# Moving the third set of table rows, one query load and the running maxima inside the prologue of a relative-position attention kernel

## The chip, the cores and the metric

One core of a Trainium2 chip runs the whole program. The metric is the device time of the program in microseconds, the median over runs. The engines are PE (TensorE), DVE (VectorE), ACT (ScalarE), POOL (GpSimd) and SP (SyncE, which here does nothing but issue DMAs). Each runs its own list of instructions in order; semaphores order them against each other and against the 16 DMA engines.

## The reference, cut to what matters

A decoder layer on x (4 x 1024 x 256): self-attention with 16 heads of 16 and clipped relative positions, cross-attention to a context of 154 rows, and a gated feed-forward part with quantised weights; each is added to its input and normalised. The change touches only the self-attention:

```python
q, k, v = proj(Wq, bq), proj(Wk, bk), proj(Wv, bv)
attn = einsum('bhld,bhrd->bhlr', q, k) * scale
dist = clip(arange(L)[None, :] - arange(L)[:, None], -64, 8) + 64
rel = einsum('bhld,lrd->bhlr', q, dist_emb[dist]) * scale
out = einsum('bhlr,bhrd->bhld', softmax(attn + rel), v)
```

## The kernel before, in words

The self-attention has 16 groups of four heads (`NIT`, index i, four for each batch entry) and each is done in two half groups T = 2i and 2i + 1 of 512 queries, so there are 32 half groups. All work before the half groups is the prologue, and the change lies in it.

The prologue goes over 8 blocks k of 512 rows of x (`BLKS`), and in each over six products n: two for q (n = 0, 1), two for k (2, 3), two for v (4, 5). A product (k, n) is written (4, 2) and so on below. `project` is PE's part. For n < 4, ACT makes the high bf16 part (`high`), DVE the remainder (`remainder`), ACT the middle part, POOL the low part (`low`), and SP stores the three parts to DRAM with two DMAs of 192 KB (`store_part`; L268, and L270 for small wrapped pieces of 3 KB in even blocks). For v, ACT copies, POOL adds the bias and SP stores 544 KB (`store_values`). PE has two PSUM banks for this, so a product waits for DVE (`a_rem`) or ACT (`a_vc`) to have read the one two before it. The SBUF buffers of parts and values are double: `high(k, n)` waits until the stores of block k - 2 have landed.

Between the products stands the early work of the first half groups:

- `load_q(i)`, four DMAs of 768 KB together, brings the stacked parts of q of group i; `load_k`, `load_v` and `load_max_operands` bring the other operands.
- Rows (T, j), j = 0 to 3: PE multiplies q by the position embedding (`make_row`, L810; it waits for `load_q` of group T // 2), ACT copies, POOL pads, SP stores 400 KB to a table in DRAM (`store_row`, L326). When all four have landed, `load_windows(T)` reads them back skewed, in four DMAs of 400 KB (L318).
- Chunks (T, c), c = 0 to 15: PE multiplies q and k roughly (`max_chunk`, L836 and L837, into one of two banks) and DVE takes maxima with the window added (`chunk`, L710 to L715; the first of a half group waits for its window). 24 chunks are done in the prologue, 16 for T = 0 and 8 for T = 1.
- `shift_of(T)` on POOL, `turn_shift(T)` on PE and `place_shift(T)` on SP (L331) turn the maxima of a half group into three extra rows of q. Half group 0 can't begin without them.

The tables `rows_after` and `chunk_after` say behind which product a row or a chunk stands, on every engine alike. SP's list is written out by hand. In before it goes through blocks 3 and 4 with `load_windows(0)`, `load_q(1)`, the rows of T = 1, `load_windows(1)` and the rows of T = 2 in between, then stores blocks 5 and 6, and then issues `place_shift(0)`, `load_windows(2)`, `load_max_operands(1)`, `load_v(0)` and the stores of block 7, in this order. Behind that begins the loop over half groups. In its first half group PE needs `place_shift(0)` for the first score (`scores`, L866), and `load_v(0)` for the first product with v (`weigh`, L884), which stands behind the scores of two key tiles.

Of the kernel before, what the change touches and what calls it, by code (L numbers as in the profile page):

```python
# [45 lines left out]
def self_attention(nc, sem, ad, xT, wqT, wkT, wvT, bq, bk, bv, emb, part_of_row, e_lo, e_hi, ident,  # L46
# [17 lines left out]
    BLKS = 2 * B  # L64
# [5 lines left out]
    with ctx:  # L70
# [149 lines left out]
        steps = [(k, n) for k in range(BLKS) for n in range(6)]  # L220
        rows_after = {s_: (0, j) for j, s_ in enumerate(((2, 4), (2, 5), (3, 0), (3, 1)))}
        rows_after.update({(3, 2 + j): (1, j) for j in range(4)})
        rows_after.update({(4, 2 + j): (2, j) for j in range(4)})
        first_chunks = [(0, c) for c in range(CH)] + [(1, c) for c in range(LEAD)]
        chunk_after = dict(zip(steps[steps.index((4, 0)):], first_chunks))
        SHIFT_STEP = (7, 0)

        def chunks_of(T, kt):

# [7 lines left out]
        def q_slot(i):  # L237
            return i % QS
# [5 lines left out]
        def _(sp):  # L244
# [16 lines left out]
            def store_part(k, n):  # L261
                b, hf = k // 2, k % 2
                cols = slice(hf * HALF, (hf + 1) * HALF)
                sp.wait_ge(a_low, 4 * k + n + 1)
                for gg in range(2):
                    dst = (qd, kd)[n // 2][4 * b + 2 * (n % 2) + gg].rearrange("t r h n -> (r h) t n")
                    src = part[gg * G * HD:(gg + 1) * G * HD, hf, n]
                    sp.dma_start(dst[:, :, cols], src).then_inc(st_part[hf][n], 16)  # L268
                    if n >= 2 and hf == 0:
                        sp.dma_start(dst[:, :, L:L + WRAP], src[:, :, 0:WRAP]).then_inc(st_part[hf][n], 16)  # L270

            def store_values(k):
                b, hf = k // 2, k % 2
                cols = slice(hf * HALF, (hf + 1) * HALF)
                sp.wait_ge(a_v, 2 * k + 2)
                sp.dma_start(vd[b, cols].rearrange("(t p) c -> p t c", p=P), vs[:, hf].rearrange("p t h r -> p t (h r)")).then_inc(st_val[hf], 16)
                if hf == 0:
                    sp.dma_start(vd[b, L:L + WRAP], vs[0:WRAP, hf, 0].rearrange("p h r -> p (h r)")).then_inc(st_val[hf], 16)

            def three(t, i, p0, p1, lo, hi):  # L280

                return t[i, p0:p1].rearrange("t r h n -> (t r) h n")[:, :, lo:hi]

            def load_q(i):
                q, s = qT[:, q_slot(i)], ld_q[q_slot(i)]
                sp.dma_start(q[0:16], three(qd, i, 0, 1, 0, L)).then_inc(s, 16)
                sp.dma_start(q[16:48], three(qd, i, 0, 2, 0, L)).then_inc(s, 16)
                sp.dma_start(q[48:80], three(qd, i, 1, 3, 0, L)).then_inc(s, 16)
                sp.dma_start(q[80:96], three(qd, i, 0, 1, 0, L)).then_inc(s, 16)
# [62 lines left out]
            def store_parts(k, *projections):  # L352
                for n in projections:
                    store_part(k, n)

            def store_rows(T, *tiles):
                for j in tiles:
                    store_row(T, j)
# [17 lines left out]
            store_parts(3, 1)  # L376
            sp.wait_ge(s_pads, 16 * 2 * ENDS)
            load_windows(0)
            load_q(1)
            store_rows(1, 0)  # L380
            store_parts(3, 2)
            store_rows(1, 1)
# [2 lines left out]
            store_values(3)  # L385
            store_parts(4, 0, 1)
            load_windows(1)
            store_rows(2, 0)
            store_parts(4, 2)
            store_rows(2, 1)  # L390
            store_parts(4, 3)
            store_rows(2, 2, 3)
            store_values(4)
            load_k(0)
            sp.wait_ge(s_bufs, 1 + 2 * G)
            for par in range(2):
                sp.dma_start(kT[99:102, par, :, (TL - 1) * P:L - WRAP], none[0:3, :, 0:P - WRAP]).then_inc(s_wrap, 16)
            for k in range(5, BLKS - 1):
                store_parts(k, 0, 1, 2, 3)
                store_values(k)  # L400
            place_shift(0)
            load_windows(2)
            load_max_operands(1)
# [53 lines left out]
        def _(pool):  # L457
# [12 lines left out]
            def low(k, n):  # L470

                hf = k % 2
                pool.wait_ge(a_mid, 4 * k + 1 + n)
                nc.gpsimd.tensor_tensor(part[:, hf, n, 2, :], rem[:, hf, n, :], part[:, hf, n, 1, :], ALU.subtract).then_inc(a_low, 1)  # L474
# [48 lines left out]
            for k, n in steps:  # L523
                if (k, n) == (0, 4):
                    pool.wait_ge(s_const, 16 * NCONST)
                    pool.wait_ge(s_ones, 1)
                if n < 4:
                    low(k, n)
                else:
                    add_value_bias(k, n - 4)  # L530
                if (k, n) in rows_after:
                    pad_row(*rows_after[k, n])
                if (k, n) == (6, 4):
                    shift_of(0)
                    fill_ends(0)
                    cut_window(0)
# [20 lines left out]
        def _(act):  # L557
# [66 lines left out]
            for k, n in steps:  # L624
# [8 lines left out]
                if (k, n) in rows_after:  # L633
                    copy_row(*rows_after[k, n])
                if (k, n) == SHIFT_STEP:
                    copy_shift(0)
# [18 lines left out]
        def _(dve):  # L655
# [40 lines left out]
            def chunk(T, c):  # L696

                q4, h, n = c // G, c % G, CH * T + c
                qt = 4 * (T % 2) + q4
                a, z = max(0, qt * P - LEFT), min(L, qt * P + P + RIGHT)  # L700
                u = a - (qt * P + RIGHT - P)
                bank = psX[:, n % 2, :]
                if c == 0:
                    dve.wait_ge(ld_w[T % NW], 16 * G * (T // NW + 1))
                    if T >= 2:
                        dve.wait_ge(m_top, T - 1)
                if n >= 2:
                    dve.wait_ge(x_read, n - 1)
                dve.wait_ge(x_full, n + 1)
                last = nc.vector.tensor_tensor_reduce(junk[:, n % 2, 0:z - a], bank[:, a:z], win[:, T % NW, q4, h, u:u + z - a],  # L710
                                                      1.0, NEG, ALU.add, ALU.max, mx[:, T % 2, q4, h, 1:2])
                if a > 0:
                    last = nc.vector.tensor_reduce(mx[:, T % 2, q4, h, 0:1], bank[:, 0:a], AX.X, ALU.max)  # L713
                if z < L:
                    last = nc.vector.tensor_reduce(mx[:, T % 2, q4, h, 2:3], bank[:, z:L], AX.X, ALU.max)  # L715
                last.then_inc(x_read, 1)
                if c == CH - 1:
                    dve.wait_ge(x_read, n + 1)
                    nc.vector.tensor_tensor(mx[:, T % 2, :, :, 3], mx[:, T % 2, :, :, 0], win[:, T % NW, :, :, FLAT], ALU.add).then_inc(m_left, 1)
                    if T:  # L720
                        dve.wait_ge(m_ready, T)
                    dve.wait_ge(m_left, T + 1)
                    nc.vector.tensor_reduce(shift[:, 0], mx[:, T % 2].rearrange("p q h s -> p (q h) s")[:, :, 1:4], AX.X, ALU.max).then_inc(m_top, 1)
# [19 lines left out]
            for k, n in steps:  # L743
                if n < 4:
                    remainder(k, n)
                if (k, n) == (0, 5):
                    dve.wait_ge(s_const, 16 * NCONST)
                    prepare_embedding()
                    nc.vector.memset(none[:], 0.0).then_inc(s_bufs, 1)
                if k in (2, 3) and n < 4:  # L750
                    ones_row(k - 2, n)
                if (k, n) in chunk_after:
                    chunk(*chunk_after[k, n])
            dve.wait_ge(a_vc, 2 * BLKS)
            nc.vector.memset(psO[:], 0.0).then_inc(s_bufs, 1)
            for T in range(NT):
# [13 lines left out]
        def _(pe):  # L770
# [57 lines left out]
            def max_chunk(T, c):  # L828
                i, q4, h, n = T // 2, c // G, c % G, CH * T + c
                if c == 0:  # L830
                    pe.wait_ge(ld_q[q_slot(i)], q_loads(i))
                    pe.wait_ge(ld_x[i % 2], 16 * 7 * (i // 2 + 1))
                if n >= 2:
                    pe.wait_ge(x_read, n - 1)
                lo = T % 2 * HALF + q4 * P
                mm(psX[:, n % 2, 0:HALF], qT[0:64, q_slot(i), h, lo:lo + P], kX[0:64, i % 2, h, :], start=True, stop=True)  # L836
                mm(psX[:, n % 2, HALF:L], qX[64:128, i % 2, h, lo:lo + P], kX[64:128, i % 2, h, :], start=True,  # L837
                   stop=True).then_inc(x_full, 1)
# [49 lines left out]
            for k, n in steps:  # L888
                project(k, n)
                if (k, n) == (2, 4):  # L890
                    pe.wait_ge(s_prep, 3)
                if (k, n) in rows_after:
                    make_row(*rows_after[k, n])
                if (k, n) in chunk_after:
                    max_chunk(*chunk_after[k, n])
                if (k, n) == SHIFT_STEP:
                    turn_shift(0)
            pe.wait_ge(a_rem, 4 * BLKS)
# [1179 lines left out]
```

## Time and profile before

| what | value |
|---|---|
| median of 3 runs | 1418.46 us (1417.92 to 1419.0) |
| the profiled execution, own time | 1418.14 us |
| its span, first to last instruction | 1416.4 us |
| PE busy | 89% of the span |
| DVE, ACT, POOL busy | 75%, 69%, 25% |
| prologue, up to the first score | 129.1 us |
| half groups 0 to 31 | from there to about 960 us |

In the page's picture of the span in 40 slices of 35.4 us, PE shows 9 or more tenths from slice 5 on to slice 27, and 7 to 8 in the first four. The DMA engines show 7 to 9 tenths in the first five slices, more than in any later slice. A DMA share near 1.1 in the views below is a full queue, since packets of one DMA engine overlap.

### The profile page before, as it was taken

To read this page: it belongs to the slowest core of one execution; us is meant where nothing else is said; L and a number is where in the kernel's file an instruction comes from. 1 tells how busy PE (TensorE), PEld (TensorE's weight loads), DVE (VectorE), ACT (ScalarE), POOL (GpSimd) and SP (SyncE) were. 2 spreads that over 40 slices of the span, in tenths; PEclk is the share of its full clock that TensorE was granted. 3 is DMA by queue.
4 is the path that set the end of the run, shared out by engine and by line. 5 is a ranking of instruction groups with operands and counts; after the bars stand their busy time and mean duration, and the time that the engine had idled before them with its cause. 6 is when DMAs were issued, how large, how long until landed. Compare 5 with 4: busy or idle time off the path is not lost. (4 is left out here: it accounts for less than half of the span.)

```text
span 1416.4 us, 25656 instructions
## 1 busy us (share of the span) xinstructions
PE 1257.9 (89%) x8540; PEld 672.4 (47%) x8540; DVE 1057.2 (75%) x2561; ACT 974.5 (69%) x1690; POOL 352.5 (25%) x587
## 2 busy tenths in 40 slices
PE   7788999999999999999999999999997699930397
PEld 4344344334334334334434434436886588720397
DVE  3366788888887888888888888872564466999687
ACT  4434777777777777777777777772676458969672
POOL 4544121211211211212112112014463002410033
PEclk9989999999999999999999999999998899975699
DMA  8999877777777687587686685625320322837023
GB/s 221 287 305 265 204 178 202 187 183 199 185 198 188 176 216 184 158 229 182 169 219 177 186 199 156 186 79 174 103 77 34 116 89 79 276 121 267 0 90 119
DMA packets 263761, 243.02 MB, mean 172 GB/s; under 512 B 69294, under 2 KB 246990, under 8 KB 259534
## 3 DMA queue, kind: packets, MB, share of 16 engines
q1 hardware_dynamic: 261998, 238.24, 61.7%
q10 hardware_dynamic: 1632, 3.15, 0.7%
q8 instruction: 68, 1.11, 0.3%
q14 instruction: 63, 0.52, 0.1%
HBM read 139.01 MB, written 101.53 MB: 170 GB/s over the span
## 5 line engine op out<-in xcount | busy, mean ns | idle before, releaser
L618 ACT ACTIVATE pr<-scoresT 128x512 f32<-128x512 f32 x1024 | 548.4, 600 | 205.7 <-PE scoresT L871 148.9
L866 PE MATMUL scoresT<-qT,kT 99*128 99x512 bf16 (+9 forms) x1536 | 357.4, 313 | 4.8 <-issue 2.3
L715 DVE TENSOR_REDUCE mx<-scores_for_max 128x1 f32<-128x888 f32 (+6 forms) x448 | 301.6, 673 | 0.0
L710 DVE CUSTOM_DVE_ANT_0 junk<-scores_for_max,win 128x200 f32<-128x200 f32 (+2 forms) x512 | 179.9, 351 | 152.9 <-PE scores_for_max L837 144.2
L713 DVE TENSOR_REDUCE mx<-scores_for_max 128x1 f32<-128x64 f32 (+6 forms) x448 | 277.4, 619 | 0.0
L884 PE MATMUL attn_out<-pr,vS 128*17 128x512 f32 x2048 | 270.3, 600 | 2.5 <-DMA vS<-v_all 2.3
L866 PEld LDWEIGHTS scoresT<-qT,kT 99*128 99x128 bf16 (+1 forms) x1536 | 113.2, 98 | 334.0 <-ACT rows L595 97.0
L871 PE MATMUL scoresT<-idf,win 128*128 128x128 f32 (+1 forms) x1024 | 199.6, 256 | 0.0
L836 PE MATMUL scores_for_max<-kX,qT 64*128 64x512 bf16 x512 | 167.8, 386 | 3.9 <-DVE mx L715 3.0
L484 POOL COPY rows<-rows 128x512 f32<-128x512 f32 x128 | 78.6, 614 | 361.3 <-ACT rows L595 361.3
L837 PE MATMUL scores_for_max<-kX,qX 64*128 64x512 bf16 x512 | 167.8, 386 | 0.0
L871 PEld LDWEIGHTS scoresT<-idf,win 128*128 128x128 f32 (+1 forms) x1024 | 128.1, 143 | 19.2 <-issue 0.5
L2003 PE MATMUL banks<-w_gate_high,x_high 128*128 128x256 f32 x128 | 36.8, 288 | 82.5 <-DVE x_low L1925 82.4
L1869 DVE TENSOR_REDUCE amax<-raw 128x1 f32<-128x3072 f32 (+2 forms) x26 | 80.6, 3100 | 5.9 <-ACT raw L1772 5.6
L836 PEld LDWEIGHTS scores_for_max<-kX,qT 64*128 64x128 bf16 x512 | 35.9, 94 | 100.7 <-issue 47.2
L2003 PEld LDWEIGHTS banks<-w_gate_high,x_high 128*128 128x128 f32 x128 | 25.2, 197 | 83.1 <-issue 82.8
L595 ACT ACTIVATE rows<-scoresT 128x288 f32<-128x288 f32 x128 | 54.2, 424 | 10.8 <-DMA rel_table<-rows 10.2
L1772 ACT ACTIVATE raw<-banks,step 128x512 f32<-128x512 f32 x48 | 33.1, 689 | 29.2 <-PE banks L1978 29.2
L810 PE MATMUL scoresT<-embS,qT 96*128 96x72 bf16 x512 | 37.9, 196 | 16.8 <-DMA qT<-q_parts 10.4
L474 POOL TENSOR_TENSOR shared<-rem,shared 128x512 bf16<-128x512 f32 x32 | 36.8, 1157 | 59.0 <-ACT shared L571 58.9
L884 PEld LDWEIGHTS attn_out<-pr,vS 128*17 128x17 f32 x2048 | 34.0, 95 | 34.4 <-ACT pr L618 10.5
L519 POOL TENSOR_TENSOR shared<-ov,orec 128x256 f32<-128x256 f32 x16 | 10.0, 623 | 148.1 <-PE scoresT L866 106.8
(219 smaller groups left out, 2005.5 us busy)
## 6 DMA issues: line engine op xcount, KB each, us to landing
rel_table<-rows SPq DMA_DIRECT2D x128, 400.0 KB, 4.1
win<-rel_table SPq DMA_DIRECT2D x128, 400.0 KB, 5.0
up_raw<-xT_normed SPq DMA_DIRECT2D x6, 1536.0 KB, 10.3
xT_normed<-up_raw SPq DMA_DIRECT2D x6, 1536.0 KB, 6.4
qT<-q_parts SPq DMA_DIRECT2D x32, 256.0 KB, 7.1
kX<-k_parts SPq DMA_DIRECT2D x64, 128.0 KB, 4.1
kT<-k_parts SPq DMA_DIRECT2D x32, 256.0 KB, 4.8
q_parts<-shared SPq DMA_DIRECT2D x32, 192.0 KB, 4.5
```

Source lines behind the costliest of these rows:

```text
L484: nc.gpsimd.tensor_copy(rows[:, j, :, 0:LP], rows[:, j, :, LP:LP + 1].to_broadcast([P, G, LP])).then_inc(r_padded, 1)
L618: nc.scalar.activation(pr[:, n % NPR, h, :], bank, ACT.Exp).then_inc(t_read, 1)
L710: last = nc.vector.tensor_tensor_reduce(junk[:, n % 2, 0:z - a], bank[:, a:z], win[:, T % NW, q4, h, u:u + z - a], 1.0, NEG, ALU.add, ALU. ...
L713: last = nc.vector.tensor_reduce(mx[:, T % 2, q4, h, 0:1], bank[:, 0:a], AX.X, ALU.max)
L715: last = nc.vector.tensor_reduce(mx[:, T % 2, q4, h, 2:3], bank[:, z:L], AX.X, ALU.max)
L836: mm(psX[:, n % 2, 0:HALF], qT[0:64, q_slot(i), h, lo:lo + P], kX[0:64, i % 2, h, :], start=True, stop=True)
L837: mm(psX[:, n % 2, HALF:L], qX[64:128, i % 2, h, lo:lo + P], kX[64:128, i % 2, h, :], start=True, stop=True).then_inc(x_full, 1)
L866: last = mm(bank[:, a:e], k[0:r], q[0:r, a:e], start=(n == 0), stop=not near and n == len(pieces) - 1, skip_group_check=True)
L871: last = mm(bank[:, a:e], rel, idf[0:e - a, 0:e - a], is_transpose=True, start=False, stop=n == len(near) - 1, skip_group_check=True)
L884: last = mm(psO[32 * h:32 * h + VW, :], vS[:, i % 2, kt, VW * h:VW * (h + 1)], pr[:, n % NPR, h, :], start=(kt == 0), stop=(kt == TL - 1))
L1869: nc.vector.tensor_reduce(amax[:, k, n:n + 1], src, AX.X, ALU.max, apply_absolute_value=True).then_inc(done, 1)
L2003: mm(to(n, q), oh[m // 2][:, c], wdh[:, d], start=(m == 0 and q % 2 == 0), stop=False, skip_group_check=True)
```

## The change

It moves work between places of the prologue and leaves every instruction as it is.

- `rows_after`: the four rows of T = 2 stand behind the products (6, 2) to (6, 5) in place of (4, 2) to (4, 5).
- Chunks: they begin behind (4, 4) in place of (4, 0). At (5, 4), (5, 5), (6, 4) and (6, 5) two are done in place of one, so that all 24 are still done by (7, 5).
- `SHIFT_STEP` and POOL's `shift_of(0)` come one product later, (7, 1) and (6, 5).
- SP: `load_q(1)` stands behind `load_k(0)`, in front of the stores of block 5, in place of behind `load_windows(0)`. The four `store_row(2, j)` stand among the stores of the second half of block 6, the last of them right in front of `place_shift(0)` and `load_windows(2)`.

```diff
-        rows_after.update({(4, 2 + j): (2, j) for j in range(4)})
+        rows_after.update({(6, 2 + j): (2, j) for j in range(4)})
-        chunk_after = dict(zip(steps[steps.index((4, 0)):], first_chunks))
-        SHIFT_STEP = (7, 0)
+        TWICE = [(k, n) for k in (5, 6) for n in (4, 5)]
+        chunk_steps = sorted(steps[steps.index((4, 4)):] + TWICE)
+        chunks_after = {s_: [c for at, c in zip(chunk_steps, first_chunks) if at == s_] for s_ in chunk_steps}
+        SHIFT_STEP = (7, 1)
...
             load_windows(0)
-            load_q(1)
             store_rows(1, 0)
...
             load_windows(1)
-            store_rows(2, 0)
-            store_parts(4, 2)
-            store_rows(2, 1)
-            store_parts(4, 3)
-            store_rows(2, 2, 3)
+            store_parts(4, 2, 3)
             store_values(4)
             load_k(0)
...
-            for k in range(5, BLKS - 1):
-                store_parts(k, 0, 1, 2, 3)
-                store_values(k)
+            load_q(1)
+            store_parts(5, 0, 1, 2, 3)
+            store_values(5)
+            store_parts(6, 0, 1, 2)
+            store_rows(2, 0)
+            store_parts(6, 3)
+            store_rows(2, 1, 2)
+            store_values(6)
+            store_rows(2, 3)
             place_shift(0)
             load_windows(2)
...
-                if (k, n) == (6, 4):
+                if (k, n) == (6, 5):
                     shift_of(0)
```

PE in block 4, before: behind the first product of k, (4, 2), stands the first row of T = 2 (`embS,qT`), which waits for `load_q(1)` (`ld_q1`), and a chunk (`scores_for_max`).

```order
L788 MATMUL scoresT<-xs,wk 128x512 [waits a_rem]
L788 MATMUL scoresT<-xs,wk 128x512
L810 MATMUL scoresT<-embS,qT 128x72 [waits t_read,ld_q1]
L810 MATMUL scoresT<-embS,qT 128x72 x3
L836 MATMUL scores_for_max<-kX,qT 128x512 [waits x_read]
L837 MATMUL scores_for_max<-kX,qX 128x512
L788 MATMUL attn_out<-xs,wk 128x512 [waits a_rem]
```

PE at the same place, after: the products of q and k in block 4 follow each other, and the first chunk stands behind (4, 4).

```order
L791 MATMUL scoresT<-xs,wk 128x512 [waits a_rem]
L791 MATMUL scoresT<-xs,wk 128x512
L791 MATMUL attn_out<-xs,wk 128x512 [waits a_rem]
L791 MATMUL attn_out<-xs,wk 128x512
L796 MATMUL scoresT<-wv,xs 128x256 [waits a_rem]
L796 MATMUL scoresT<-wv,xs 128x256 x3
L839 MATMUL scores_for_max<-kX,qT 128x512 [waits ld_x0,ld_q0]
```

Nothing that waits for `ld_q1` is left in block 4.

SP behind the stores of block 6, before: the last store of k's parts, the values, then the shift and the third window.

```order
L268 DMA k_parts<-shared 64x3x512
L270 DMA k_parts<-shared 64x3x8
L276 DMA v_all<-vs 128x4x272 [waits a_v]
L278 DMA v_all<-vs 8x272
L331 DMA qT<-sh 6x512 [waits t_read]
L331 DMA qT<-sh 6x512 x3
L318 DMA win<-rel_table 128x4x200 [waits st_row2,st_row3,st_row1,st_row0]
```

SP at the same place, after:

```order
L328 DMA rel_table<-rows 128x4x200 [waits ld_w0,r_padded] x2
L278 DMA v_all<-vs 128x4x272 [waits a_v]
L280 DMA v_all<-vs 8x272
L328 DMA rel_table<-rows 128x4x200 [waits ld_w0,r_padded]
L333 DMA qT<-sh 6x512 [waits t_read]
L333 DMA qT<-sh 6x512 x3
L320 DMA win<-rel_table 128x4x200 [waits st_row2,st_row3,st_row1,st_row0]
```

The rows of T = 2 now stand here, and the third window waits for the landing of a store that is issued just ahead of it.

## Rows read from the trace of the kernel before

**Rows 1.** The page, its first line and the busy times.

```profile
span 1416.4 us, 25656 instructions
PE 1257.9 (89%) x8540; PEld 672.4 (47%) x8540; DVE 1057.2 (75%) x2561; ACT 974.5 (69%) x1690; POOL 352.5 (25%) x587
```

**Rows 2.** Waits, 60 to 240 us: us in total, times, longest.

```profile
DVE junk L710 <- DMA win<-rel_table: 7.7, 1, 7.7
...
PE scoresT L810 <- DMA qT<-q_parts: 9.2, 1, 9.2
...
PE scoresT L866 <- issue: 2.3, 1, 2.3
PE attn_out L884 <- DMA vS<-v_all: 2.3, 1, 2.3
```

**Rows 3.** Timeline of block 4: start, us, engine, line; idle before and releaser.

```profile
64.64 1.98 PE L788 MATMUL scoresT<-xs,wk 128*128 128x512 f32 x4
...
72.12 0.30 DVE L710 CUSTOM_DVE_ANT_0 junk<-scores_for_max,win 128x136 f32<-128x136 f32 x1 [7.72 <-DMA win<-rel_table]
...
75.81 0.42 PE L810 MATMUL scoresT<-embS,qT 96*128 96x72 bf16 x4 [9.18 <-DMA qT<-q_parts]
```

**Rows 4.** Timeline, products on PE: two of block 1, two of block 6.

```profile
18.57 1.88 PE L788 MATMUL scoresT<-xs,wq 128*128 128x512 f32 x4
...
20.29 1.88 PE L788 MATMUL attn_out<-xs,wq 128*128 128x512 f32 x4
...
101.87 1.98 PE L788 MATMUL attn_out<-xs,wq 128*128 128x512 f32 x4
...
104.11 1.98 PE L788 MATMUL scoresT<-xs,wk 128*128 128x512 f32 x4
```

**Rows 5.** Timeline, two chunks in a row on DVE, their first instructions.

```profile
112.21 0.37 DVE L710 CUSTOM_DVE_ANT_0 junk<-scores_for_max,win 128x200 f32<-128x200 f32 x1
...
113.49 0.35 DVE L710 CUSTOM_DVE_ANT_0 junk<-scores_for_max,win 128x200 f32<-128x200 f32 x1
```

**Rows 6.** Stretches: us, PE, PEld, DVE, ACT, POOL busy, clock, DMA share, GB/s.

```profile
66.00:114.00 48.00, 38.82 (x136) 18.66 (x135) 31.34 (x80) 17.91 (x31) 22.11 (x24) 0.89 1.09 317
114.00:122.00 8.00, 8.00 (x27) 2.79 (x25) 6.29 (x16) 3.59 (x6) 5.33 (x8) 1.00 0.80 213
122.00:124.00 2.00, 2.00 (x10) 1.44 (x8) 1.79 (x6) 1.58 (x3) 0.92 (x2) 1.00 0.06 13
```

**Rows 7.** Stretches with TensorE's granted clock (last but two), same columns.

```profile
72.00:76.00 4.00, 0.20 (x4) 0.20 (x4) 3.83 (x8) 0.63 (x1) 1.15 (x1) 0.50 0.99 249
76.00:82.00 6.00, 6.00 (x19) 2.57 (x17) 1.94 (x4) 1.84 (x4) 0.14 (x1) 0.52 1.11 324
...
140.00:150.00 10.00, 10.00 (x55) 3.51 (x53) 5.13 (x13) 5.44 (x11) 0.85 (x2) 0.67 0.86 200
```

**Rows 8.** Timeline of SP: start, us spent on issuing.

```profile
62.55 2.55 SPq L318 DMA_DIRECT2D win<-rel_table  x4
...
83.17 2.40 SPq L318 DMA_DIRECT2D win<-rel_table  x4
...
109.55 3.64 SPq L268 DMA_DIRECT2D q_parts<-shared  x4
113.24 0.66 SPq L268 DMA_DIRECT2D k_parts<-shared  x1
...
119.73 2.99 SPq L331 DMA_DIRECT2D qT<-sh  x4
122.90 2.02 SPq L318 DMA_DIRECT2D win<-rel_table  x4
...
129.50 0.38 SPq L310 DMA_DIRECT2D vS<-v_all  x1
```

**Rows 9.** Timeline, PE's first score and first product with v.

```profile
129.09 0.38 PE L866 MATMUL scoresT<-qT,kT 99*128 99x200 bf16 x2 [2.31 <-issue]
...
138.16 1.05 PE L884 MATMUL attn_out<-pr,vS 128*17 128x512 f32 x8 [2.31 <-DMA vS<-v_all]
```

**Rows 10.** The row stores, 40 to 145 us: issue to landing.

```profile
DMA to landing us min/median/max: 4.6/6.3/10.4
```

More of the change, by code:

```diff
@@ L751, in _ @@
                     ones_row(k - 2, n)
-                if (k, n) in chunk_after:
-                    chunk(*chunk_after[k, n])
+                for c in chunks_after.get((k, n), ()):
+                    chunk(*c)
             dve.wait_ge(a_vc, 2 * BLKS)
@@ L893, in _ @@
                     make_row(*rows_after[k, n])
-                if (k, n) in chunk_after:
-                    max_chunk(*chunk_after[k, n])
+                for c in chunks_after.get((k, n), ()):
+                    max_chunk(*c)
                 if (k, n) == SHIFT_STEP:
```

## The prediction

> **What bounds the kernel now.** I read the page first, then the waits, then the stretches and the timeline of the prologue, SP's row of the timeline last. The page [rows 1] says that PE is busy 89% of the span; in the slices of the page between the prologue and the end of the half groups it is 9 tenths or more. The change leaves all that work alone, so it can win only what PE loses before the half groups run, and the question is by how much the point moves from which PE runs without a stop.
>
> The waits of this part [rows 2] name three losses of PE: 9.2 us for `load_q(1)`, 2.3 us at the first score, 2.3 us for `load_v(0)`. The first is what the change goes at. In the timeline [rows 3] PE makes the product (4, 2) at 64.64, then sits until 75.81 before the first row of T = 2. DVE sits 7.7 us too, until the first window lands at 72.12, and the maxima of the first chunk and the remainder of (4, 1) are queued behind it. After the stop the clock is at half (granted 0.50 and 0.52, the 1.2 GHz level) up to 82 us [rows 7].
>
> PE isn't the only thing that is full here. From 66 to 114 us the DMA engines have a share of 1.09 and move 317 GB/s; from 114 to 122 the share is 0.80 and the rate 213; from 122 to 124 nearly nothing moves [rows 6]. SP shows why: it issues without a pause from 109.55 to 122.9 [rows 8], about 0.65 us for each DMA, and eight of the last ones before 119.7 are the small wrapped pieces of k and the values, four more are the shift. So up to 114 the queue is bound by what it moves, and then for 9 us by SP.
>
> The last wait sets the end. The first score comes at 129.09, and the first product with v at 138.16, released by the DMA of vS [rows 9]. That load is issued at 129.50, behind `load_windows(2)` at 122.90 and `load_max_operands(1)` [rows 8]. From the issue of window 2 to PE's release are 138.16 - 122.90 = 15.3 us. Whatever PE gains earlier, it waits there.
>
> **Removed: the wait for `load_q(1)`, and with it what PE did late.** From the product (4, 2) at 64.64 there are 22 products to the end of the prologue. One alone takes 20.29 - 18.57 = 1.72 us, one with a chunk 104.11 - 101.87 = 2.24 us, so a chunk adds 0.52 [rows 4]. With four rows at 0.15 (an estimate from their four short products) PE needs 22 x 1.72 + 24 x 0.52 + 0.6 = 50.9 us and ends at about 115.5. In before it ends at 126.8 (129.09 less 2.31 idle). That is 11.3 us for PE alone: 9.2 of wait, the rest from the slow clock.
>
> The part buffers could hold this back, since `high(k, n)` waits for the stores of two blocks earlier. Without the 768 KB of `load_q(1)`, which took the queue from 72.12 to 75.81, 3.7 us [rows 3], and without the four rows of T = 2 (1.6 MB, 5 us at 317 GB/s), the stores of block 4 come some 4 us earlier by the queue and k's 5 to 8; those of block 5 are again behind `load_q(1)`. By the queue's rate I put the first store of block 5 at about 103.5 landed, where ACT wants it at 103.3, and the later ones ahead of their use. I take a stall of 0 to 2 us, hidden by what follows.
>
> **Chunks doubled.** DVE takes 113.49 - 112.21 = 1.28 us for a chunk [rows 5]. In a block with two doubled steps it has 8 x 1.28 + 4 x 0.75 = 13.2 us of work, and PE 6 x 1.72 + 8 x 0.52 = 14.5. DVE lags by half a microsecond behind a doubled step and makes it up in the next. Cost 0 to 1 us in all, hidden as well. `turn_shift` and `shift_of` one product later cost nothing: SP gets to the shift at 113 or later, its data are ready by about 106.
>
> **The DMA queue, which is the sum.** All that the queue has to move before `load_windows(2)` is the same set of transfers in both kernels, since `load_q(1)` and the rows of T = 2 were moved ahead of that point within it, not past it. The queue is full from 66 us on. So it ends earlier only by the time in which it was not full. Between 114 and 122 it moved 8 x 213 = 1.70 MB, which at 317 GB/s is 5.4 us: 2.6 us idle in effect; by the share, 8 x (1.09 - 0.80) / 1.09 = 2.1 us. From about 122.0 to 122.9 it was empty, another 0.9 us [rows 6, 8]. In the changed kernel the rows of T = 2, 400 KB each, stand between the small pieces, so that the queue stays full while SP issues them. All data for them are there: the last row's product comes at about 101.5. SP's own time isn't in the way either: from the second window on (in after at about 79.6: 83.17 less 3.7) it has to issue some 35 us of DMAs and would end at 115. The queue then runs empty at 122.0 - 2.6 = 119.4.
>
> **The added wait.** `load_windows(2)` now waits for the row (2, 3), which is stored just ahead of the shift. Behind that wait on SP stand `load_max_operands(1)`, `load_v(0)` and all stores of block 7; PE's first product with v waits for them. With a full queue a row lands when the queue has got to it, so I count only its tail, 0 to 1.5 us, and take 0.5, as the median row lands 6.3 us after issue and SP is about that far ahead of the queue [rows 10]. Window 2 is then issued at 119.4 + 0.5 = 119.9, 3.0 us earlier than before. Ends: 2.1 - 0.6 = 1.5 us on the low side, 2.6 + 0.9 = 3.5 on the high one.
>
> Nothing behind window 2 changes, so vS lands at about 135.2. The shift lands at about 120, since its DMAs stand in the full queue; PE, ready at 115.5, starts the half group then, is at the first product with v at about 127 and waits 8 us there, in place of 2.3. Of the 11.3 us that PE gains 3.0 are left.
>
> **The clock behind that wait.** In before the clock falls after the 2.3 us of idle time: granted 0.67 from 140 to 150 [rows 7]. After the 9.2 us stop it was at half for 5.9 us of work, 75.8 to about 81.7. A wait of 8 us should be like the second, so I book the same loss for both kernels, and half a microsecond either way.
>
> **Sum.** 1418.14 of the profiled execution less 3.0 is 1415.1; it lies 0.3 under the median of the runs, so the forecast is **1415.4 us**. 0.2% of the time is 2.8 us, about what a measurement can tell from no change, so the forecast lies just outside of it.
>
> **Rivals.**
>
> A, *SP sets the end and not the queue*. If the queue catches up before block 6 ends, window 2 is issued when SP gets there, at 115 to 117, and the gain is 6 to 8 us: 1411. For it speaks that SP was what held the queue from 114 on [rows 6, 8]. Against it speaks the share of 1.09 over 48 us, and that the changed kernel has 1.6 MB more to move in just that stretch of SP's list. Chance 0.13. The Trainium skill, "Perfetto Trace Analysis", section "What 'DMA-bound' means", keeps two bounds apart: the DMA engines themselves, or the sequencer of the issuing engine, which then shows a solid track of DMA slices. SP's track is solid from 109.55 on, so by that rule this rival would be the forecast; the share of 1.09 up to 114 goes against it.
>
> B, *the queue loses as much as it gains*. The 8 KB packets of `load_q(1)`, moved next to `load_k(0)`, or a starved moment at the second window, which waits for the rows of T = 1, cost 1 to 2 us of rate; or the last row's tail is 1.5 us and more. Then 0 to 1.4 us are left: 1417 to 1418.5. Chance 0.17.
>
> C, *the wait for the last row takes the place of the removed one*: slower. The row (2, 3) is issued directly ahead of the shift. If SP gets there no earlier than it got to the shift in before (119.73 [rows 8]), the row is issued at 119.7, lands 6.3 us later [rows 10] at 126.0 to 126.6 with nothing else in the queue, window 2 is issued 3 to 4 us later than at 122.90, and the time is 1422. It decides if block 6 comes 6 us or more later than I have it, say by stalls on part buffers. Chance 0.08.
>
> D, *PE's whole gain stays*, 1407: only if vS landed by 127, for which its place in SP's list leaves no room. Below 0.01, and not counted.
>
> **Chances and range.** The forecast's own case, a gain of 2 to 5 us, has 0.62: 0.40 of it is beyond 0.2%, 0.22 within. With A, faster is 0.53; with B, same is 0.39; slower is 0.08. The own range is 1413.4 to 1416.5. The range to 1411.5 takes in half of A, and up to 1418.9 all of B; left out are C and the rest of A, about 0.15.
>
> **What would show it.** Right: no wait for `qT<-q_parts` in block 4, products at 1.7 to 2.0 us up to (4, 3), PE through with the prologue at 114 to 118, window 2 issued at 119 to 121, DMA share above 1 from 66 to 119, a wait of 6 to 9 us on vS before the first product with v, which comes at 134.5 to 136.5. Wrong: window 2 issued before 118 (A) or after 122 (B, C), PE stopped in blocks 5 to 7 by `st_part`, or a stop in half group 1 or 2 that before doesn't have.

## The result and the profile after

The changed kernel takes 1422.42 us (median of 19 runs, 1420.44 to 1425.17), the kernel before 1419.36 (median of 19, 1417.43 to 1422.66). The ratio is 1.0019, with a 95% interval of 1.0013 to 1.0026: slower by 0.19%, or 2.7 us (1.8 to 3.7). The forecast was 1415.4, and the range ended at 1418.9; both lie on the wrong side. The profiled execution took 1420.71 us with a span of 1418.9, against 1418.14 and 1416.4 before. The ratios below use fast executions alone; one of e1's twelve took 2400.79 us and is left out.

The page of the changed kernel, its first line and the busy times, answers [rows 1]. The number of instructions and the work are the same:

```profile
span 1418.9 us, 25656 instructions
PE 1255.3 (88%) x8540; PEld 672.2 (47%) x8540; DVE 1057.1 (75%) x2561; ACT 973.7 (69%) x1690; POOL 354.4 (25%) x587
```

PE's waits from 60 to 240 us (total, times, longest) answer [rows 2]:

```profile
PE scoresT L813 <- DMA qT<-q_parts: 9.8, 1, 9.8
PE attn_out L887 <- DMA vS<-v_all: 5.3, 1, 5.3
PE scoresT L869 <- issue: 2.3, 1, 2.3
PE scoresT L869 <- DMA qT<-sh: 1.0, 1, 1.0
```

The wait for the second stacked q is still there, and longer than the 9.2 us of before. It stands at another place, as PE's timeline shows (start, us; idle before it and releaser in brackets), which answers [rows 3]:

```profile
64.42 1.98 PE L791 MATMUL scoresT<-xs,wk 128*128 128x512 f32 x4 [0.22 <-DVE rem L696]
66.24 1.88 PE L791 MATMUL attn_out<-xs,wk 128*128 128x512 f32 x4
68.10 1.99 PE L796 MATMUL scoresT<-wv,xs 128*128 128x256 f32 x8
...
91.59 1.98 PE L791 MATMUL scoresT<-xs,wk 128*128 128x512 f32 x4
103.37 0.42 PE L813 MATMUL scoresT<-embS,qT 96*128 96x72 bf16 x4 [9.79 <-DMA qT<-q_parts]
103.72 0.60 PE L839 MATMUL scores_for_max<-kX,qT 64*128 64x512 bf16 x1
104.26 3.78 PE L791 MATMUL attn_out<-xs,wk 128*128 128x512 f32 x4
```

In block 4 the products now follow each other as forecast. PE is through with (6, 2) at 93.57, and the row behind it, the first one of T = 2, stands until 103.37. SP's timeline says why, and answers [rows 8]:

```profile
62.53 2.28 SPq L320 DMA_DIRECT2D win<-rel_table  x4
...
80.77 2.60 SPq L320 DMA_DIRECT2D win<-rel_table  x4
...
94.22 1.67 SPq L394 DMA_DIRECT2D kT<-no_shift  x2
95.94 0.42 SPq L288 DMA_DIRECT2D qT<-q_parts  x1
...
97.36 0.42 SPq L291 DMA_DIRECT2D qT<-q_parts  x1
97.83 2.63 SPq L270 DMA_DIRECT2D q_parts<-shared  x4
...
103.83 3.56 SPq L270 DMA_DIRECT2D q_parts<-shared  x4
110.60 0.57 SPq L270 DMA_DIRECT2D k_parts<-shared  x1
...
119.87 0.92 SPq L328 DMA_DIRECT2D rel_table<-rows  x1
120.83 3.33 SPq L333 DMA_DIRECT2D qT<-sh  x4
125.63 2.02 SPq L320 DMA_DIRECT2D win<-rel_table  x4
...
132.14 0.38 SPq L312 DMA_DIRECT2D vS<-v_all  x1
```

`load_q(1)` is issued from 95.94 on, 2.4 us after PE began to want it, and lands at 103.3. The same stop then reaches SP. It has issued the q parts of block 6 at 107.39 and stands until 110.60 for the k parts of (6, 2), although PE had made that product at 93.57. ACT and POOL tell where it lay:

```profile
93.67 0.69 ACT L569 ACTIVATE shared<-scoresT,colc 128x512 bf16<-128x512 f32 x1 [1.03 <-PE scoresT L791]
94.26 0.62 ACT L574 ACTIVATE shared<-rem 128x512 bf16<-128x512 f32 x1
103.82 0.41 ACT L598 ACTIVATE rows<-scoresT 128x288 f32<-128x288 f32 x1 [8.95 <-PE scoresT L813]
108.14 0.69 ACT L569 ACTIVATE shared<-attn_out,colc 128x512 bf16<-128x512 f32 x1 [3.90 <-PE attn_out L791]
108.72 0.62 ACT L574 ACTIVATE shared<-rem 128x512 bf16<-128x512 f32 x1
...
109.42 1.16 POOL L477 TENSOR_TENSOR shared<-rem,shared 128x512 bf16<-128x512 f32 x1 [13.31 <-ACT shared L574]
```

ACT makes the middle part of a product one product later, behind the copy of the row (L598) and the next high part. So the finished product (6, 2) waits for the row that waits for `load_q(1)`, and its store is issued 17 us after PE was done with it.

Four stretches answer [rows 6, 7] (PE, PEld, DVE, ACT and POOL busy, granted clock, DMA share, GB/s):

```profile
96.00:106.00 10.00, 2.63 (x8) 1.19 (x9) 1.37 (x4) 0.41 (x1) 0.10 (x1) 0.61 1.06 267
106.00:114.00 8.00, 7.86 (x41) 4.64 (x39) 4.77 (x14) 3.67 (x8) 4.58 (x6) 0.85 0.76 222
114.00:122.00 8.00, 8.00 (x26) 3.01 (x27) 7.49 (x21) 3.64 (x7) 6.09 (x11) 1.00 0.95 278
124.00:126.00 2.00, 2.00 (x11) 1.31 (x10) 1.99 (x6) 1.59 (x3) 1.50 (x2) 1.00 0.06 16
```

From 106 to 114 the queue has a share of 0.76: it ran dry while SP stood from 107.39 to 110.60 (0.12 from 110 to 112). After PE's stop the clock is at its lower level (1.2 GHz, granted 0.50 from 104.26 to 108.04), and the product (6, 3) takes 3.78 us in place of 1.98.

The end of the prologue answers [rows 9]:

```profile
130.25 0.38 PE L869 MATMUL scoresT<-qT,kT 99*128 99x200 bf16 x2 [2.32 <-issue]
141.13 1.91 PE L887 MATMUL attn_out<-pr,vS 128*17 128x512 f32 x8 [5.32 <-DMA vS<-v_all]
```

Window 2 is issued at 125.63 in place of 122.90, 2.7 us later, v's load with it, and the first product with v comes 3.0 us later. The first half group ends 2.6 us later than before, the last one 2.8. That is the result.

### The profile page after: what moved, and what is told of

The parts are those of the page before. It is cut to its first block and busy times, and to the rows that moved or that the text cites. A ratio compares the mean times of both kernels' runs of the same rounds, so it can differ in the third digit from the quotient of the medians.

```text
span 1418.9 us, 25656 instructions
## 1 busy us (share of the span) xinstructions
PE 1255.3 (88%) x8540; PEld 672.2 (47%) x8540; DVE 1057.1 (75%) x2561; ACT 973.7 (69%) x1690; POOL 354.4 (25%) x587
## 5 line engine op out<-in xcount | busy, mean ns | idle before, releaser
L598 ACT ACTIVATE rows<-scoresT 128x288 f32<-128x288 f32 x128 | 54.4, 425 | 17.8 <-PE scoresT L813 10.0
L813 PE MATMUL scoresT<-embS,qT 96*128 96x72 bf16 x512 | 37.9, 196 | 18.1 <-DMA qT<-q_parts 11.5
L477 POOL TENSOR_TENSOR shared<-rem,shared 128x512 bf16<-128x512 f32 x32 | 36.8, 1155 | 58.8 <-ACT shared L574 58.6
```

## The experiments

Two executions don't reach the prologue's middle at the same time, so places are compared as distances from the issue of the first window, in us. All are differences of starts in the timelines. "Half group 0 ends" is ACT's first copy of a half group's output. Ratios are to the kernel before in runs beside it, with 95% intervals. Each row of places is one profiled execution; e4 and e7 have the same SP list up to window 2 and differ there by 0.8 us (61.5 and 60.7), so a difference under 1 us is read as nothing unless a wait in the profile accounts for it.

| kernel | PE ends prologue | window 2 issued | first score | first product with v | half group 0 ends | ratio |
|---|---|---|---|---|---|---|
| before | 64.2 | 60.3 | 66.5 | 75.6 | 102.4 | |
| the change | 65.4 | 63.1 | 67.7 | 78.6 | 104.9 | 1.0019 [1.0013, 1.0026] |
| e1, q back | 55.4 | 62.2 | 63.3 | 76.1 | 102.9 | 1.0011 [1.0000, 1.0021] |
| e2, rows alone | 61.9 | 61.2 | 64.2 | 76.9 | 103.5 | 1.0004 [0.9992, 1.0017] |
| e3, maxima alone | 65.5 | 61.0 | 67.9 | 75.7 | 102.4 | 1.0008 [0.9998, 1.0018] |
| e4, before, v early | 64.3 | 61.5 | 66.6 | 73.3 | 102.3 | 1.0007 [0.9997, 1.0018] |
| e5, e1 without 4 DMAs | 55.6 | 60.5 | 61.5 | 74.9 | 101.8 | 0.9995 [0.9985, 1.0004] |
| e6, before without them | 63.8 | 58.6 | 66.1 | 72.8 | 101.3 | 0.9997 [0.9987, 1.0007] |
| e7, e4, loads moved | 64.3 | 60.7 | 66.6 | 73.3 | 96.3 | 0.9945 [0.9926, 0.9963] |
| e8, e1, same edits | 55.2 | 61.7 | 63.0 | 69.8 | 93.6 | 0.9939 [0.9925, 0.9954] |
| e9, e8, shift first | 55.5 | 63.5 | 57.8 | 65.6 | 96.6 | 0.9970 [0.9959, 0.9981] |
| e10, the change, same edits | 67.0 | 64.7 | 69.3 | 75.7 | 98.8 | 0.9961 [0.9949, 0.9973] |

**e1: is it the place of `load_q(1)`?** The change with this load back where it was.

```diff
             load_windows(0)
+            load_q(1)
...
-            load_q(1)
             store_parts(5, 0, 1, 2, 3)
```

> The changed kernel with load_q(1) put back behind load_windows(0), where it stood in before; rows of T = 2, maxima and shift as in the change. Theory 1 (the wait for load_q(1) was moved, not removed: in the changed kernel PE stood 9.79 us for it before the row behind (6, 2), and that made blocks 6 and 7, window 2 and vS late): no wait for qT<-q_parts in the prologue, window 2 issued at 119 to 121 us in place of 125.6, first product with v at 134.5 to 136.5, and 1.5 to 3.5 us less than the kernel before. Theory 2 (the last row's landing in front of window 2 costs by itself): window 2 still at 124 or later and a time of 1 to 3 us above before.

No wait for the second q is left, and PE is through with the prologue 8.9 us sooner than before. Of these, nothing arrives. PE's waits, 60 to 240 us:

```profile
PE scoresT L869 <- issue: 7.9, 1, 7.9
PE attn_out L887 <- DMA vS<-v_all: 5.9, 1, 5.9
PE scores_for_max L839 <- DVE mx L718: 2.2, 2, 1.2
```

And SP's timeline, from window 1 on:

```profile
86.89 2.41 SPq L320 DMA_DIRECT2D win<-rel_table  x4
...
101.24 2.62 SPq L270 DMA_DIRECT2D q_parts<-shared  x4
...
122.71 3.23 SPq L333 DMA_DIRECT2D qT<-sh  x4
126.45 2.01 SPq L320 DMA_DIRECT2D win<-rel_table  x4
```

Between these SP issues almost without a pause. From the stores of block 5 to window 2 are 25.2 us, where it was 19.5 before (103.43 to 122.90), because the rows of T = 2 now stand there (2.7 us of issuing) and some other DMAs take longer to issue. But the list as a whole is no longer for that. From window 1 to window 2 SP has the same 51 DMAs in both kernels and takes 39.6 us in e1 and 39.7 before, 37.4 and 37.9 of them spent on issuing. The 1.9 us by which window 2 comes later in e1 lie before window 1, which is issued at 22.7 in place of 20.6; e5, e8 and e9, which share these edits, show 22.2 to 23.1. What makes it late wasn't separated.

So the late q costs the 2.0 us of half group 0 by which the change (104.9) lies behind e1 (102.9), and without it nothing is won all the same: SP's list is the next bound. The times don't tell the two apart (1.0019 and 1.0011, with overlapping intervals). Of the expectation, Theory 1 got the wait right and window 2 and the time wrong. Theory 2 got both numbers, but not the cause: SP waits only 0.4 us for the last row.

**e2 and e3: the two other parts alone.** e2 moves the rows of T = 2 in before as the change does, on every engine, and leaves the rest. e3 takes the chunks, `SHIFT_STEP` and `shift_of(0)` of the change and leaves rows and loads.

```diff
# e2
-        rows_after.update({(4, 2 + j): (2, j) for j in range(4)})
+        rows_after.update({(6, 2 + j): (2, j) for j in range(4)})
# e3
-        chunk_after = dict(zip(steps[steps.index((4, 0)):], first_chunks))
-        SHIFT_STEP = (7, 0)
+        SHIFT_STEP = (7, 1)
```

> The kernel before with the rows of T = 2 alone moved behind block 6 (and SP's stores of them); load_q(1) and the maxima as in before. Theory 1: PE has no stop on load_q(1), but DVE stands until window 0 lands near 72 us with the remainder of (4, 1) queued behind it, so PE stands about 7 us at (4, 3); since the DMA queue sets the end, window 2 is still issued at 119 to 121.5 and the gain is 1.5 to 3.5 us, nearly that of the run with load_q(1) put back. Theory 2: 1 to 3 us above before.

> The kernel before with the maxima and the shift alone moved (begun behind (4, 4), twice doubled). Theory 1: PE stands about 10 us for load_q(1) at (4, 2) as in before, since the rows of T = 2 are still there; the end of the prologue within 1 us of before and the time within 1 us (0.1%). Theory 3 (the doubled steps and the later shift cost something): 1 to 2 us more than before.

In e2 the wait for q is gone, and PE stops at the same place for the other reason that had stood behind it: both banks of the chunks are full until the first window lands.

```profile
73.66 0.61 PE L837 MATMUL scores_for_max<-kX,qT 64*128 64x512 bf16 x1 [6.76 <-DVE mx L716]
```

Window 2 comes 0.8 us later and the end of half group 0 1.1 us; SP's wait for the last row's landing in front of window 2, 1.3 us by the profile, accounts for it. Theory 1 had PE's stop (about 7 us), but neither window 2 nor the gain. In e3 that end is where it was before (102.4 both). Doubling chunks costs PE two waits of 0.4 us for DVE. The shift one product later is not free, as the prediction had it: SP stands 0.9 us for ACT's copy of it. Nothing of this reaches the end of half group 0. The ratios of e2 and e3 aren't apart from 1.

**e5 and e6: SP's issuing or the queue?** Both take four small wrapped pieces of k in block 6, 12 KB together, out of SP's last stretch; e5 is e1 so changed, e6 is before. The pieces are written from zeros early in the prologue, so the wrapped columns of k of the last batch entry aren't computed.

```diff
-                    if n >= 2 and hf == 0:
+                    if n >= 2 and hf == 0 and k < 6:
```

> The run with load_q(1) put back, with the four wrapped pieces of 3 KB of block 6 taken out of SP's list there; they are written earlier, in front of load_windows(0), from a tile of zeros (so k's 8 wrapped columns of the last batch are left zero). Times are counted from the issue of window 0, since that differs by 1.5 us between runs. Theory S (from the stores of block 5 on SP's own issuing, 0.65 us a DMA, sets when window 2 goes, so that the four rows put into this stretch cost their issue): window 2 at +59 to +60.5 us in place of +62.2, 1.8 to 3 us earlier though only 12 KB less are moved, and vS as much earlier. Theory Q (the bytes in the queue set it, as in my forecast): unchanged within 0.5 us.

> The kernel before with the same four pieces taken out of block 6. Theory S: window 2 at +57.5 to +58.8 us from window 0 in place of +60.35, vS lands 1.5 to 2.6 us earlier and PE's 2.3 us wait for it nearly goes, but the time falls by under 1 us, since PE gets to its first product with v only 2.3 us before vS and the shift of T = 1 then ends the first half group. Theory Q: window 2 unchanged within 0.5 us.

If the queue's bytes set the end, 12 KB are worth nothing. Window 2 moved by 1.7 us in both (62.2 to 60.5 and 60.3 to 58.6); in e6 0.5 us of it lies before the stores of block 5, where nothing was taken out. Four DMAs at 0.65 us would be 2.6. Part of the rest is waits that come up in its place: 1.6 us for the values of block 6 in e6, 0.9 us for the last row in e5 (0.4 in e1). Both places lie where Theory S had them. So the bytes are not the bound, and SP's time for each DMA, some 0.6 us even for 3 KB, fits what was seen. One rival isn't separated by these runs. The pieces are many small packets (from 114 to 122 us, 959 packets under 512 bytes in before), and the DMA engines' time for them went too. Against it speaks that the engines weren't full there: their share is 0.80 in before and 0.84 in e1, where a full queue shows 1.05 or more. In e6 the first product with v comes 2.8 us earlier, and 1.1 us of this is left at the end of half group 0. Something in that half group takes the rest.

**e4: v alone.** In before, `load_v(0)` behind `load_k(0)`, 27 us earlier; its place in the scratch memory overlapped with a tile of zeros, which for this got room of its own.

```diff
+            load_v(0)          # behind load_k(0)
...
-            load_v(0)          # behind load_max_operands(1)
```

> The kernel before with load_v(0) alone issued behind load_k(0) in place of behind load_max_operands(1); to allow it the tile 'zero' is 128 bytes longer, so that vS lies on it alone. Theory 4 (vS sets the start of the half groups): PE's 2.3 us wait for vS at 138 us is gone, and with it a stretch of half clock; 2.3 to 5 us less than before. Rival: the 2.7 us of queue time that vS took are given back earlier or at the first score, and the next wait (window 2's operands, the shift of T = 1) takes over: within 1 us of before.

The wait for v is gone, and PE makes the first product with it 2.3 us sooner. The end of half group 0 is at 102.3, where it was before (102.4), as the rival of the expectation had it. PE and SP, timeline:

```profile
160.25 0.97 PE L865 MATMUL scoresT<-qT,kT 102*128 102x512 bf16 x3 [4.54 <-DMA qT<-sh]
...
137.11 0.95 SPq L326 DMA_DIRECT2D rel_table<-rows  x1
143.72 0.57 SPq L293 DMA_DIRECT2D kT<-k_parts  x1
...
150.95 2.97 SPq L331 DMA_DIRECT2D qT<-sh  x4
```

The scores of T = 1 wait for their shift. SP issues it at 150.95, behind a stop of 5.7 us (138.06 to 143.72), in which it waits for the last stored parts and values, and behind nine loads and three rows. The vS wait was not the only thing that set the end, though the prediction took it so.

**e7, e8 and e10: both bounds taken away.** e7 is e4, e8 is e1 with v early, e10 the change as made with v early. In each the list in the first half group is changed too: `load_k(1)` and `load_v(1)` behind `place_shift(1)`, and SP's wait for the last stored values at T = 2 in place of T = 0.

```diff
-                    if kt == 1 and T == 0:
+                    if kt == 1 and T == 2:
...
                         place_shift(T + 1)
+                        if T == 0:
+                            load_k(1)
+                            load_v(1)
```

> The kernel before with load_v(0) behind load_k(0), as in the run with that alone, and in the first half group load_k(1) and load_v(1) behind place_shift(1) and the wait for the stores of block 7 moved to T = 2. Theory E (SP's list in the first half group is the next bound: with load_v(0) early PE stood 4.54 us for the shift of T = 1, which landed 5 us after its issue behind those loads): that wait goes, half group 0 ends 3 to 5 us earlier from window 0 on, and the time is 2.5 to 4.5 us under before. Rival: another load of T = 1 or T = 2 (k, the windows, q of group 2) takes over and less than 1 us is left.

> The same two edits to loads, on the changed kernel with load_q(1) put back behind load_windows(0). Theory E: here PE is through with the prologue some 9 us earlier than in before, so with vS and the loads out of the way the shift of T = 0 (landed about 62 us after window 0) sets the start; half group 0 ends 4 to 7 us earlier than in before and the time is 4 to 7 us under before, 1 to 3 us under the run with the loads moved in before. Rival: as there.

> The change as it was made (load_q(1) behind load_k(0)) with the two edits of e8 in the first half group: v of half group 0 early, load_k(1) and load_v(1) behind place_shift(1), the wait for the stored values at T = 2. Theory (the wait for load_q(1) was moved from (4,2) to (6,2), not removed): TensorE stops some 9 to 10 us at (6,2) for the second stacked q, its prologue ends at window 0 + 65 in place of e8's + 55.2, and the time is 1 to 4 us above e8. Rival (the late q is hidden behind SyncE's list, which only ends at + 58): within 1 us of e8.

e7 is 0.55% faster than before, e8 0.61%; between the two, run side by side, the times (1413.46 and 1411.98) can't tell, while half group 0 ends 2.8 us sooner in e8. It ends 6.0 and 8.8 us sooner than before, both more than was expected (3 to 5 and 4 to 7). Whether the moved loads or the moved wait for the stored values gave it was not tried. e10 shows what the place of `load_q(1)` costs where nothing behind it covers for it:

```profile
106.23 0.42 PE L814 MATMUL scoresT<-embS,qT 96*128 96x72 bf16 x4 [11.85 <-DMA qT<-q_parts]
132.62 0.38 PE L870 MATMUL scoresT<-qT,kT 99*128 99x200 bf16 x2 [2.32 <-issue]
```

Half group 0 ends at 98.8 against 93.6, 5.2 us later than in e8 and 2.4 later than in e7, which has nothing of the change. The ratio of 0.9961 lies 0.2% above e8's; they ran on different chips, and the intervals overlap a little (from 0.9949 and up to 0.9954), so that here the places in the table carry the verdict.

**e9: the shift first.** In e8 PE stands 7.8 us before the first score. ACT begins to copy the shift at 109.1, and SP issues it at 120.60, behind three rows and the values.

```diff
             store_parts(6, 3)
+            place_shift(0)
             store_rows(2, 1, 2)
...
             store_rows(2, 3)
-            place_shift(0)
```

> The kernel of e8 (the change with load_q(1) behind load_windows(0), v of half group 0 loaded early, load_k(1) and load_v(1) behind place_shift(1), the wait for the stored values at T = 2), and in it place_shift(0) in front of store_rows(2,1,2), store_values(6) and store_row(2,3), directly behind the k parts of (6,3). In e8 ScalarE had copied the shift at 109.10, SyncE issued its copy into place at 120.60, and TensorE stood 7.76 us before the first score. Theory (the order of SyncE's list sets the first score): the first score comes 2.3 us behind the end of the prologue on TensorE, at window 0 + 57.5 to 59 in place of + 62.96, half group 0 ends 3 to 5 us sooner than e8's + 93.55, and the time is 3 to 5 us below e8. Rival (window 2, which comes as late as before or 0.8 us later, takes over): the first score is early, the stop comes back in front of T = 2, and under 1.5 us is left.

The first half of the theory held: the first score came at 57.8 in place of 63.0. The second didn't; half group 0 ends 3.1 us later than in e8, and 0.9970 is worse than 0.9939. PE's timeline:

```profile
139.37 0.37 PE L840 MATMUL scores_for_max<-kX,qT 64*128 64x512 bf16 x1 [3.61 <-issue]
...
154.55 0.82 PE L870 MATMUL scoresT<-qT,kT 102*128 102x512 bf16 x3 [2.97 <-DMA qT<-sh]
```

PE comes early to the first chunk of T = 2, whose operands SP loads with window 2, 1.7 us later than in e8, and then waits again for the shift of T = 1. Why window 2 is late stands in SP's timeline:

```profile
121.05 0.88 SPq L328 DMA_DIRECT2D rel_table<-rows  x1
125.17 2.01 SPq L320 DMA_DIRECT2D win<-rel_table  x4
```

Window 2 waits for the landing of the last row, and the shift's 3 us of issuing, which covered most of that wait in e8, no longer stand between the two: SP stands 3.2 us. The rival that stood in the expectation won, and by more than it said: it had left a small gain. That the operands are what the first of these waits is for is read from the order of the work; the profile names no releaser, and no run separates it.

## Why the prediction was wrong

**Removed wait: wrong, and here the forecast fell.** The step says that `load_q(1)`'s wait goes. It went from (4, 2) to (6, 2) together with the row that needs it. The prediction had both numbers and didn't put them side by side. By its own durations PE is at the first row of T = 2 at 93.2, which is 64.64 + 13 x 1.72 + 12 x 0.52 (measured 93.6). By its own account of the queue the stores behind `load_q(1)` land at about 103.5 (the load itself landed at 103.3). A load that is moved later along with its user must be checked against its user's new time, and here that check gives a stop of 10 us. It gives also the second effect, ACT's middle part of (6, 2) behind the copy of the waiting row, and so SP's empty 3.2 us.

**Part buffers and doubled chunks: nearly right.** In e1, where PE doesn't stop for q, ACT waits 0.7 to 2.8 us four times for stores of two blocks earlier, and PE ends the prologue at 55.4; the forecast from the issue of window 0 was 53.0, so the stall is 2.4 us where the range ended at 2. Chunks cost PE one wait of 0.4 us in the change, two of 0.4 in e3 and two of 1.0 and 1.2 in e1. The later shift was booked at nothing: in e3 SP waits 0.9 us for it.

**The sum by the queue: wrong, also without the first error.** The step took the transfers' bytes for the bound up to 119 and said that SP's own time "isn't in the way", since it would end at 115. In e1 nothing stops SP for long and window 2 is issued at 62.2, where the step had 57.3 (119.9 less 62.55). e5 and e6 speak against bytes: 12 KB less, 1.7 us sooner. The term that was mis-sized is SP's own list. The step counted some 35 us from window 1 to window 2. SP took 44.9 us in the change: 38.4 on issuing 55 DMAs (0.70 each), 3.2 for the k parts of (6, 2), 1.5 in front of window 2, the rest in short gaps. The rows had it: before took 122.90 less 83.17, 39.7 us, over the same list without the four loads of `load_q(1)` [rows 8]. With these (1.9 us) and from 79.6 on, that puts window 2 at 121.2 at the best. In the run from 109.55 to 122.90 are 18 DMAs, 0.74 us each and not 0.65, and the pieces and values in it are six, not eight. Two sentences of the prediction pointed the right way: SP issues without a pause from 109.55 [rows 8], and the Trainium skill ("Perfetto Trace Analysis", section "What 'DMA-bound' means") names the issuing sequencer as a bound of its own where its track is solid. By that rule the prediction made a rival of it, A, but gave it a gain of 6 to 8 us, as if SP then got there by 117. The rule holds here, by SP's nearly solid list in e1 and by e5 and e6; A's price doesn't, since all of these DMAs stand in SP's list in either kernel, and moving them about in it makes it no shorter.

**The added wait: right in kind, 1.3 us more than before in place of 0.5.** The shift's DMAs end at 124.16 and window 2 follows at 125.63, 1.5 us later, where before it was 0.2. The row (2, 3), issued at 119.87, was still under way.

**What stands behind window 2: half right.** v's load came 6.5 us behind window 2 (6.6 before), and PE waited for it, 5.3 us where the step had 8. But e4 shows that in before this wait hid the list behind it: v loaded in time gave nothing until the loads in front of `place_shift(1)` and the wait for the stored values were moved too (e7). So the 3 us of the forecast would hardly have become 3 us of time; in e6 v came 2.8 us sooner, and 1.1 was left. The clock behind that wait was booked alike for both kernels, and that held: from the first product with v to the end of half group 0 are 26.8 us before and 26.3 after.

**The rivals.** C had the time (1422) and the condition: SP at the last row at 119.7 (it was 119.87), block 6 later by 6 us or more. It got 0.08, because its cause was sought in part buffers and not in the load itself. A named the engine that did set the end, with the wrong sign, and B came out for the queue with too small a loss. With the place of q put right (e1) the ratio is 1.0011, so there would have been no gain even then.

## What to carry to other kernels

When a load and its first user are both moved, write down for both kernels when the load lands and when the user is reached; a wait that disappears from one place is looked for at the other before it is counted as won. Where one engine issues every DMA, keep a second sum beside the bytes: the time that this engine took, in the trace, for the list that ends in the critical load. Moving a DMA within that list doesn't shorten it. A wait in the profile names what came last, not the only thing that is late: here v was to be early and three edits farther on had to follow before anything was gained (e4 against e7 and e8).

## What the runs showed of the hardware

A DMA of 3 KB can hold SP as long as one of 192 KB, 0.6 us each: the lines of block 4 in the changed kernel show both side by side.

```profile
87.80 0.61 SPq L272 DMA_DIRECT2D k_parts<-shared  x1
88.45 0.61 SPq L270 DMA_DIRECT2D k_parts<-shared  x1
```

Both have 64 x 3 rows, of 8 and of 512 numbers. So the length of the rows doesn't set this time; whether their count does wasn't tried. It isn't the same for all shapes: each load of `load_q(1)` took 0.42 to 0.45 us.

The time of one kernel moves between executions by as much as most of these edits are worth or more. The eight executions of e9 go from 1410.88 us at a mean granted clock of 0.957 to 1418.38 at 0.950. In the profiled executions the stretch from the end of half group 0 to that of half group 31 takes 793.6 to 794.9 us in every kernel, while the part behind it takes from 456.8 (e9) to 461.3 (e5), with the same instructions. What sets it wasn't tried. So the verdicts above rest on the places in the table and the intervals together, and differences of a microsecond in time (e2, e3, e5, e6) are left as not told apart.
